# A four-part transformer stack on one core: matmul banks shared as three pairs and one single bank, with another order of steps

## What is computed

```python
x = x + 0.5 * _L0_ffn_ref(_layernorm(x), ...)     # stage A: three cycles of a gated "twist"
x = x + _L0_attn_ref(_layernorm(x), ...)          # stage B: causal attention, 16 heads, latent keys, rope
x = x + 0.5 * _L0_ffn_ref(_layernorm(x), ...)     # stage C: as A
x = x + 0.5 * _L1_ffn_ref(_layernorm(x), ...)     # stage D: 64 features, each through a small net of 16
x = x + _L1_attn_ref(_layernorm(x), ...)          # stage E: attention with strided keys, then a 1024-wide FFN
x = x + 0.5 * _L1_ffn_ref(_layernorm(x), ...)     # stage F: as D

# one cycle of A and C (out starts as x; gf comes from a small net on the mean over tokens)
tf = sigmoid(gelu(gelu(gelu(out @ w1 + b1) @ w2 + b2) @ w3 + b3) @ w4 + b4)
coupling = 0.1 + adaptive_range * (0.7 * gf + 0.3 * tf - 0.5) * 2.0
out = out + coupling * _twist(out)                # twist: o_r, o_i, p_r, p_i -> p_r, -p_i, -o_r, o_i

# stage E, head h with stride STRIDES[h] = 1,1,2,2,2,2,4,4,4,4,8,8,8,8,16,16
k_s, v_s = k[:, h, ::stride, :], v[:, h, ::stride, :]
outs.append(softmax(q[:, h] @ k_s.T * scale) @ v_s)
```

## Time and profile before

| | us |
|---|---|
| median of 3 runs | 3855.83 |
| lowest, highest | 3854.97, 3858.72 |
| profiled execution | 3855.25 |
| its span, first to last instruction | 3853.3 |
| busy in it: PE, DVE, ACT, POOL | 3549.4, 2508.3, 1839.7, 955.4 |
| mean granted clock of PE | 0.951 |

### The profile page before, as it was taken

One profiled execution on the slowest core, in us unless ns is written; L12 is line 12 of the kernel. 1 busy time (PEld: TensorE's weight loads), 2 busy tenths in 40 slices (PEclk: granted clock), 3 DMA queues, 4 the chain that ended last, 5 costly groups with the idle time before them and its releaser, 6 DMA issues.

```text
span 3853.3 us, 57876 instructions
## 1 busy us (share of the span) xinstructions
PE 3549.4 (92%) x21952; PEld 2062.0 (54%) x21952; DVE 2508.3 (65%) x5003; ACT 1839.7 (48%) x2885; POOL 955.4 (25%) x1030
## 2 busy tenths in 40 slices
PE   2688999999999999999999999999999999999866
PEld 1344556555555655555555555655555555555433
DVE  2446576776766677676767767676767767676442
ACT  1143555546455454645545454545545464553422
POOL 0212222131323223131322313132231313222111
PEclk9798999999999999999999999999999999999977
DMA  3000000000000000000000000000000000000000
GB/s 87 1 1 1 1 1 12 1 12 1 1 12 1 12 1 12 1 1 12 1 12 1 12 1 1 12 1 12 1 12 1 7 6 1 12 1 6 1 6 6
DMA packets 39662, 27.26 MB, mean 7 GB/s; under 512 B 18464, under 2 KB 38496, under 8 KB 39392
## 3 DMA queue, kind: packets, MB, share of 16 engines
q1 hardware_dynamic: 39392, 23.56, 2.1%
HBM read 15.17 MB, written 8.39 MB: 6 GB/s over the span
## 4 chain that ended last, share of the span: by engine, by line
PE 85%; DVE 7%; ACT 4%; issue 1%; POOL 1%; DMA 0%; DVEq 0%; ACTq 0%; POOLq 0%
PE ps L494 77%; PE ps L505 8%; ACT other L1170 2%; ACT PR L1144 1%; DVE other L859 1%; DVE MX L923 1%; DVE G L961 1%; ACT L1144 1%; DVE MX L917 1%; DVE other L858 0%; DVE XN L948 0%; DVE XT L863 0%; DVE XN L902 0%; DVE XN L899 0%; DVE XN L834 0%
## 5 line engine op out<-in xcount | busy, mean ns | idle before, releaser
L1144 ACT ACTIVATE PR<-ps 128x1024 f32<-128x1024 f32 (+4 forms) x720 | 540.4, 795 | 680.6 <-PE ps L494 677.4
L494 PE MATMUL ps<-MAT 32*128 32x512 f32 (+5 forms) x4928 | 591.1, 490 | 16.4 <-ACT PR L1144 6.1
L923 DVE TENSOR_REDUCE MX<-ps 128x2 f32<-128x1024 f32 (+3 forms) x512 | 392.6, 820 | 272.0 <-PE ps L494 269.2
L1215 POOL TENSOR_TENSOR rstd<-var,neg_half 128x4 f32<-128x4 f32 x144 | 148.3, 1030 | 1216.0 <-DVE var L817 1064.9
L494 PEld LDWEIGHTS ps<-MAT 32*128 32x128 f32 (+2 forms) x4928 | 276.5, 185 | 304.0 <-issue 191.5
L494 PE MATMUL ps<-XT,cn_w 128*128 128x256 f32 x1536 | 367.0, 393 | 4.8 <-DVE XT L861 4.8
L1273 POOL TENSOR_SCALAR_AFFINE_SELECT PR<-PR 128x512 f32<-128x512 f32 x256 | 173.7, 679 | 726.2 <-ACT PR L1144 726.1
L494 PE MATMUL ps<-other,cn_w 128*128 128x512 f32 (+2 forms) x1152 | 324.3, 481 | 12.6 <-ACT other L1061 5.4
L494 PEld LDWEIGHTS ps<-XT,cn_w 128*128 128x128 f32 x1536 | 291.6, 195 | 80.1 <-issue 34.8
L494 PE MATMUL ps<-HI 32*128 32x256 f32 (+4 forms) x3072 | 221.3, 378 | 109.3 <-ACT PR L1144 74.9
L917 DVE TENSOR_REDUCE MX<-ps 128x2 f32<-128x1024 f32 (+6 forms) x256 | 220.3, 903 | 155.4 <-PE ps L494 154.8
(11 more groups left out here) (157 smaller groups left out, 6004.9 us busy)
## 6 DMA issues: line engine op xcount, KB each, us to landing
X<-in_L_attn_x SPq DMA_DIRECT2D x16, 512.0 KB, 3.9
out<-X SPq DMA_DIRECT2D x16, 512.0 KB, 2.9
w_up<-in_L_attn_W SPq DMA_DIRECT2D x1, 1024.0 KB, 7.1
w_down<-in_L_attn_W SPq DMA_DIRECT2D x1, 1024.0 KB, 8.9
w_krope<-in_L_attn_W_krope SPq DMA_DIRECT2D x1, 512.0 KB, 4.3
w_qk<-in_L_attn_Wqkv SPq DMA_DIRECT2D x4, 128.0 KB, 4.2
cn_w<-in_L_ffn_cn_w SPq DMA_DIRECT2D x1, 256.0 KB, 2.9
w_qrope<-in_L_attn_W_qrope SPq DMA_DIRECT2D x1, 256.0 KB, 4.0
```

The costliest lines, as they stand in the source:

```text
L494: return pe.matmul(dst, lhsT, rhs, start=start, stop=stop, skip_group_check=True)
L923: last = dve.tensor_reduce(MX[:, t, at], src[:, :, a:a + nk[pair]], AX_X, ALU.max)
L1144: freed(act.activation(PR[0:m, tile_of((s, q, g, kt)), 2 * pair:2 * pair + 2, q0:T], ps[0:m, b:b + 2, 0:T - q0], ACT.Exp, scale=SCALE[s]), ...
L1215: pool.tensor_tensor(rstd[:, c, :], var[:, c, :], neg_half[:], ALU.pow).then_inc(rstd_ready.sem, 1)
```

## The change

- Banks: three pairs (0,1 and 2,3 and 4,5), one single bank 6, `sum` in bank 7. xt, h1, tf, back and mout take a pair. gc, h2, h3, kvt, rope (turn), v of E, q of content in B, shift, divide, inner, up and down all take bank 6.
- Order: another table `TURN`.
- Start: X of sequence 0 and 20 small loads go first; the rest is issued in the second block, and PE and DVE wait for it ahead of the first `latent`. POOL makes the mask and clears VB, VE, MX, PR ahead of the first `h1`.
- A and C: DVE no longer keeps `ZT`; ACT turns the tanh into the coupling with one identity per half, DVE multiplies and adds with plain two-operand forms.
- B: keys come from two halves of 64 partitions (`KVT` holds two key tiles on top of each other), as do the values; q goes ahead of k.
- Mask: 32 x 32 tiles, 64 per group instead of 16 of 128 x 128.
- E: keys stand in another order (`tile_of_keys`), so that `v` needs 12 matmuls instead of 18 and four copies of ACT instead of five.

```diff
 TURN = """
-0:turn.B.2.q 0:sum.B.0.2 0:sum.B.0.3 0:content.B.2 -2:up.5 0:exp.B.1.0 -1:normal.D -2:up.6 -1:xt.D 0:max.B.2.0
+1:h2.A.2 -1:max.E.0.0 1:h3.A.2 0:xt.C -1:max.E.0.1 -1:divide.E.3 1:tf.A.2 0:h1.C.0 -1:sum.E.2.0 -1:max.E.0.2
...
+def tile_of_keys(columns, step, stride, t):
+    if stride > 4:
+        return columns[:, ::stride // step]
+    return columns[:, (0, 2, 1, 3)[t] // step::4 // step]
...
-                for dst, src in loads:
-                    sp.dma_start(dst, src, allow_slow_non_contiguous=True).then_inc(loaded, 16)
-                sp.wait_ge(loaded, ALL_LOADS)
+                sp.dma_start(X[:, 0], x_v[0]).then_inc(x_loaded[0], 16)
+                for dst, src in first_loads:
+                    sp.dma_start(dst, src, allow_slow_non_contiguous=True).then_inc(loaded_first, 16)
...
-                pairs_of_banks, single_banks, sum_bank = [0, 2], [5, 6, 7], 4
+                pairs_of_banks, single_banks, sum_bank = [0, 2, 4], [6], 7
...
+                    b = pair_bank()
                     for f in range(KT):
-                        turned(single_bank(), ("xt", s, q, f), lambda t: XN[:, q % CH, t, f * P:(f + 1) * P])
+                        turned(b + f, ("xt", s, q, f), lambda t: XN[:, q % CH, t, f * P:(f + 1) * P])
...
-                    banks = [single_bank(), single_bank()]
+                    b = pair_bank()
+                    banks = [b, b + 1]
...
-                    for t in range(TT):
-                        last = pe.transpose(dst[0:64, t * P:(t + 1) * P], LT[:, 2, 64 * t:64 * t + 64], ident[:])
+                    for t in range(2):
+                        last = pe.transpose(dst[:, t * P:(t + 1) * P], LT[:, 2, t * P:(t + 1) * P], ident[:])
...
+                    if s == "B":
+                        product(single_bank(), ("content", s, q, g, "q"), [(w_qdec[:, g, :], QL[:, q % 2, :])])
+                        b = pair_bank()
+                        dst = take(b, "content", s, q, g, "k", width=2)
+                        for v in range(2):
+                            half = slice(64 * v, 64 * v + 64)
+                            last = mm(dst[:, v, 0:T // 2], w_kdec[half, g, :], KVT[half, q % 2, :])
...
-                                last = mm(dst[:, m * C:(m + 1) * C], KVT[0:64, q % 2, t * P:(t + 1) * P], w_vdec[0:64, :])
+                                last = mm(dst[:, v, t * C:(t + 1) * C], KVT[half, q % 2, t * P:(t + 1) * P], w_vdec[half, :])
...
-                                for n in range(2):
-                                    at = first[pair] + t * P
-                                    last = mm(dst[pair][:, n, at:at + P], ident_b[:], mask_q[:], False, True)
+                                at = first[pair] + t * P
+                                for b in range(4):
+                                    for n in range(2):
+                                        row = slice(ROWS * (2 * pair + n), ROWS * (2 * pair + n + 1))
+                                        last = mm(dst[pair][ROWS * b:ROWS * b + ROWS, n, at:at + P], ident_b[row, row],
+                                                  mask_q[row, b, :], False, True)
...
-                def context_and_twist(s, q, k):
-                    dve.scalar_tensor_tensor(ZT[:, a, 0, :], XT[:, c, 1, :], gc_h[:, c, 3:4], XT[:, c, 0, :],
-                                             ALU.mult, ALU.add)
-                    link(dve.scalar_tensor_tensor(ZT[:, a, 1, :], XT[:, c, 0, :], gc_h[:, c, 3:4], XT[:, c, 1, :],
-                                                  ALU.mult, ALU.subtract))
...
-                        dve.scalar_tensor_tensor(WT[:, a, tok], TF[:, a, tok], c_tf, XT[:, c, 0, tok], ALU.mult, ALU.mult)
+                        dve.tensor_tensor(WT[:, a, tok], TF[:, a, tok], XT[:, c, 1, tok], ALU.mult)
+                        link(dve.tensor_tensor(TF[:, a, tok], TF[:, a, tok], XT[:, c, 0, tok], ALU.mult))
...
+                    for v in range(2):
+                        read_out(act, "tf", s, q, k, v)
+                        own = TF[:, area_of[s], v * T // 2:(v + 1) * T // 2]
+                        act.activation(own, own, ACT.Identity, scale=c_tf,
+                                       bias=gc_h[:, q % CH, 3:4]).then_inc(coupling_ready.sem, 1)
...
+                    if name == "latent" and a[1] == 0:
+                        prepare_rest()
```

358 lines of the change are left out of this document (191 added, 167 removed).

## The result

The change makes the kernel slower: 4042.07 us median (4041.86 to 4047.72) against 3855.4 us of before, a ratio of 1.0488 (1.047 to 1.0506). The forecast was 4010 us. The profiled execution has a span of 4040.2 us, 186.9 us more than the earlier trace rows.

The account below looks back on a forecast made before the run. PE, busy 3549.4 of 3853.3 us, was taken to bound the kernel. 3853.3 - 41 (start) + 0 (own work) + 188 (waits and clock, 12.5 x 15) + 8 (ends) = 4008 us span; forecast 4010 us, range 3870 to 4125.

Parts of the forecast that it names:

- Start: Before PE's first matmul: X and 20 small loads first let PE begin near 18.5 us; -41 us, bounds -35 and -45.
- PE's own work: PE's matmuls, weight loads and tiling-mode changes over the whole kernel: savings and costs sum near zero, bounds -8 to +79 us.
- Masks: Mask matmuls on PE: 64 tiles of 32 x 32 per group replace 16 larger ones; -20 us taken.
- switches: PE's changes between tiling modes: 356 more, at 0.19 or 0.1 us each, less exposures already there; +52 us.
- rival B: Mask matmuls: 32 x 32 tiles go at 0.029 us each, adding 81 us, 4090 us; chance 0.15.
- three direct reuses: `up.3` to `content.B.2.q`, `up.6` to `up.7`, `down.1` to `inner.D`: nothing between, 3 x 0.95 = 2.9 us per sequence.
- the largest term: `shift.B.2` waits for bank 6 until the eight relus of `inner.D` end: 4.1 us idle per sequence.
- Clock: A second long PE idle stretch per sequence brings a second stretch of half clock; 3 us per sequence.
- Ends: Where one sequence runs alone, `up.0` to `up.7` follow directly and each waits for its relu; +8 us.
- A: Bank 6 waits do not add up; idle behind `inner.F` shrinks as much, leaving the start's gain: 3815 us; chance 0.13.
- C: Only the long wait is real: 6.5 us per sequence, 98 instead of 188, 3920 us; 0.27 shared with the freed pair.
- the freed pair: Third pair frees `max.B.3.0`: 4.5 + 3 us per sequence return, 5 remain, 3900 us; 0.27 shared with C.

Follow-up runs that it names:

- The copy: Changed kernel, where ACT first copies the bank of `inner.D` and `inner.F` to SBUF and makes the eight relus from it; 4029.47 us, 13 us faster than the changed kernel.
- run 66: Not a run label: in the whole profiled run of the changed kernel, half clock took 255 us of full clock against 189 before, 66 more.

## Why the forecast was right, and where it was not

**Start.** Forecast -41, at the first matmul 60.44 to 19.84, -40.6; at the first `w_krope` -37.9. Right, within its bounds of -35 and -45.

**PE's own work.** Forecast near zero. Per middle sequence it fell by about 2: busy time 214.5 for 216.6 with order and banks of before, and 3513.7 for 3549.4 in the whole run, -36. The single terms: KVT,w_kdec went from 68.8 us in all to 46.0 (-22.8, forecast -27 with the switches), the values of B from 31.9 to 18.1 (-13.8, forecast -14), by form; the keys in the kernel before (count, busy us, mean ns):

```profile
L494 PE MATMUL ps<-KVT,w_kdec 64*128 64x512 f32 x128 | 68.8, 617 | 0.0
```

and in the changed one:

```profile
L465 PE MATMUL ps<-KVT,w_kdec 64*128 64x256 f32 x256 | 46.0, 437 | 0.0
```

Masks: forecast -20 and, as a term of its own, +52 for switches. Undone alone they cost 25 to 31 us in the changed kernel and, on the order of before, start and masks together left 0.5 us per sequence, 8 us. So rival B (0.029 us for each tile) is out: 32 tiles in 0.29 us are 0.009 each. What the prediction takes from "TensorEngine Tiling", Performance Considerations, in the Trainium skill (some 60 cycles for each matmul, by its estimate 1.6 us for 64) is contradicted by these rows, and what it takes from "TensorE: Matmul & The Clock Gate", Part 3, in the Trainium skill (starts about 4 ns apart, by its estimate a group under 0.6 us) is the nearer one: the three blocks of a group take 0.7 to 1.0 us with the switch behind each. The term mis-sized here is that for the switches, on the order of before at least: masks and switches together were put at up to +32 us, the masks with their own switches measured -8 there, and the sum of all work terms came out 36 us below zero. No run prices the switches that the changed order adds.

**Waits, the terms named.** Nearly exact, per sequence: `inner.D` to `shift.B.2` 4.1 forecast (the figures written there add up to 4.2), 37.2 / 9 = 4.13 measured; three direct reuses 2.9, measured 17.5 / 9 + 7.9 / 9 = 2.82, a small third wait of `up` in it; `turn.B.2.k` to `shift.B.1` 0.9, measured 0.99; the context's one-column steps 1.6, measured 1.78; `inner.F` and the `exp` of one pair together 0.0, measured 41.0 less 42.7 over 9, -0.19. Sum 9.5 forecast, 9.5 measured.

**Waits, the terms missed.** Idle grew by 13.3, not 9.5. The other 3.8 are h3 behind the gelu of h2 (L1074, 1.6, while the 0.6 of the old L1080 went), `mout.F` behind a row maximum 1.1 (at 1547.08), `divide` behind the copy of a `sum` 0.7, and small ones. They do not all hang on bank 6. h3 reads what that gelu writes, and `divide` turns what that copy writes. With the changed order on three single banks (the kernel with the banks of before) these waits are still there, in the nine middle sequences:

```profile
PE ps L465 <- ACT other L1069: 7.5, 18, 0.8
...
PE ps L476 <- ACT AO L1158: 6.3, 9, 0.7
```

So about half of the first (7.5 of 14.7 us) and all of the second (6.3 of 6.3) come from the order, which sets a step too soon behind the one whose result it reads, and `mout.F` waits for a pair, which it takes only since the change. I looked for pairs with nothing between them and passed those with 0.3 to 0.6 us between.

**The reason behind the largest term was only half right.** It was put down to bank 6. The copy shows that ACT's queue behind the relus is as late; the idle time moved by one step and stayed. The expectation for the copy, made in the prediction's terms (all of it the bank), was wrong by 59 us or more: 3945 to 3970 for 4029. No run moved `inner.D` away from the `exp` steps with nothing else changed.

**Clock.** Forecast 3 us per sequence. By the granted clock of the middle stretches, (1 - 0.98) x 222.3 = 4.4 us lost before and (1 - 0.95) x 239.7 = 12 after, uncertain by one or two for the rounding; by the whole run 66 / 16 = 4.1. Two kernels with the same matmuls give it from PE's busy time: 220.7 us per sequence in the changed one at a clock of 0.95, and 214.5 with order and banks of before at 0.97, 6.2 us apart (a part of that can be the switches of tiling mode that the changed order adds; no run separates the two). So 4 to 7, mis-sized by a third or more, the second term that was too small. With it the loss per sequence adds up: 13.3 of idle + 6.2 - 2.1 of own work = 17.4, where 12.5 were forecast. The prediction asked for the half clock behind the second wait; stretches of the changed kernel show it there and also where no long wait stands just ahead:

```profile
1517.50:1523.00 5.50, 5.50 (x46) 2.90 (x47) 5.39 (x11) 2.99 (x6) 1.27 (x2) 0.69 0.00 1
1547.00:1557.00 10.00, 9.43 (x125) 6.47 (x126) 7.50 (x12) 1.67 (x5) 5.45 (x5) 1.00 0.35 107
1557.00:1567.00 10.00, 10.00 (x60) 6.91 (x58) 4.27 (x15) 1.71 (x6) 1.93 (x3) 0.77 0.01 2
1567.00:1577.00 10.00, 10.00 (x84) 6.08 (x77) 1.37 (x3) 7.46 (x12) 1.91 (x3) 0.89 0.00 0
```

**How often.** Forecast 15 times 12.5, 188 us. It was 12 times 17.5 (156.5 + 53.1 = 209.6) and almost nothing (+1.2) in the turns before sequence 3. Too many turns and too few microseconds in each cancel for the most part, and that is luck: 15 x 17.5 would have been 262. In the turns before sequence 3 idle grew by 9.8 us (67.4 to 77.2) and busy time fell by 8.6; why the new waits cost nothing there stays open. Of the 32 us by which 4042 lies above 4010, the repeated part makes 23, the ends 6 and the start 3.

**Ends.** Forecast +8, measured +14.0. The step named is right; the waits of the last stretch for the relus of `up`:

```profile
PE ps L465 <- ACT other L1218: 14.8, 18, 0.9
```

**The rivals.** A (waits do not add up) is out: the two long waits stand side by side in every period, though 20 us of PE work lie between them, more than the 17 of the prediction. C (only the long wait) and the freed pair are out too; the wait behind `inner.F` is 4.06 us.

## What to carry over

Before an order of steps is planned for another sharing of banks, or a sharing for an order, both have to be timed together: each half taken back alone cost 283 or 512 us more than the pair, and the pair still lost 207 us to the old one. On a single bank a step directly behind another waited for its reader: 0.44 us behind a one-column step, 0.87 behind `up`. List every two steps of such a bank that stand close and price them; the pairs that the prediction listed came out right to 0.1 us in sum, those with half a microsecond between them were missing. List too the steps that read what the step just ahead makes, since another bank does not help these. When a bank waits for a reader, look at what else stands behind that reader in its queue before the bank is freed: here the same idle time stood one step further on.
